# Where a batch's rank products stand: one in each product's tail, or four in a row behind the last

## The reference

```python
x = x + (x @ W0.T + b0) + 2 * ((x @ A0[id0]) @ B0[id0])        # rank 16
x = x + (x @ W1.T + b1) + ((x @ A1[id1].T) @ B1[id1].T)        # rank 16
```

## Time and profile before

| | us |
|---|---|
| median of 3 runs (lowest, highest) | 282.63 (282.19, 282.70) |
| the profiled execution | 281.97 |
| its span | 280.4 |
| TensorE busy (matmuls, 1321) | 276.3 |
| VectorE busy (321) | 214.5 |
| ScalarE busy (141) | 102.0 |
| granted TensorE clock, mean of the span | 0.999 of full |

### The profile page before, as it was taken

How to read it: one execution, slowest core, us unless ns; L and a number is a source line. 1 busy time by engine, 2 the same in 40 slices (tenths; PEclk the granted TensorE clock), 3 DMA queues, 4 the chain that set the end, 5 groups by cost and what they waited for, 6 DMA issues and landing times.

```text
span 280.4 us, 3861 instructions
## 1 busy us (share of the span) xinstructions
PE 276.3 (99%) x1321; PEld 225.4 (80%) x1321; DVE 214.5 (77%) x321; ACT 102.0 (36%) x141; POOL 19.2 (7%) x45
## 2 busy tenths in 40 slices
PE   8999999999999999999999999999999999999995
PEld 6888888888888886888877888888877888888885
DVE  5779999999899799798972875875772865875413
ACT  4665465352964665404131223132311223132000
POOL 3333200400000001001000000000000000000000
PEclk9999999999999999999999999999999999999999
DMA  7997100200476200383702703703802302203003
GB/s 245 388 411 287 37 1 2 57 19 0 150 269 247 86 2 19 109 314 126 248 15 84 247 29 121 240 6 124 236 1 86 125 0 112 95 2 132 19 0 150
DMA packets 13112, 33.93 MB, mean 121 GB/s; under 512 B 2165, under 2 KB 2421, under 8 KB 13094
## 3 DMA queue, kind: packets, MB, share of 16 engines
q1 hardware_dynamic: 12066, 31.60, 31.8%
q0 software_dynamic: 1024, 2.10, 2.3%
q10 hardware_dynamic: 4, 0.00, 0.0%
HBM read 22.09 MB, written 11.60 MB: 120 GB/s over the span
## 4 chain that ended last, share of the span: by engine, by line
PE 99%; DVE 0%; issue 0%
PE bank L1291 18%; PE bank L1292 18%; PE bank L1293 18%; PE bank L1127 9%; PE bank L1131 9%; PE bank L1132 9%; PE bank L1323 3%; PE bank L1298 3%; PE bank L1159 1%; PE bank L1161 1%; PE bank L1160 1%; PE bank L1147 1%; PE bank L1146 1%; PE bank L1145 1%; PE bank L1170 1%; PE bank L1238 1%
## 5 line engine op out<-in xcount | busy, mean ns | idle before, releaser
L1291 PE MATMUL bank<-ops,late 128*128 128x512 f32 x192 | 75.1, 391 | 0.0
L1292 PE MATMUL bank<-ops,late 128*128 128x512 f32 x192 | 74.8, 390 | 0.0
L1293 PE MATMUL bank<-ops,late 128*128 128x512 f32 x192 | 74.7, 389 | 0.0
L1131 PE MATMUL bank<-ops 128*128 128x512 f32 x112 | 43.8, 391 | 0.0
L1132 PE MATMUL bank<-ops 128*128 128x512 f32 x112 | 43.6, 390 | 0.0
L1291 PEld LDWEIGHTS bank<-ops,late 128*128 128x128 f32 x192 | 36.1, 188 | 8.7 <-issue 1.2
L1293 PEld LDWEIGHTS bank<-ops,late 128*128 128x128 f32 x192 | 36.0, 188 | 7.6
L1292 PEld LDWEIGHTS bank<-ops,late 128*128 128x128 f32 x192 | 36.1, 188 | 7.4
L1127 PE MATMUL bank<-ops 128*128 128x512 f32 x112 | 40.9, 400 | 0.0
L525 ACT CAST late<-rows 128x512 fp32r<-128x512 f32 x24 | 14.7, 620 | 54.7 <-DVE rows L823 29.5
L1127 PEld LDWEIGHTS bank<-ops 128*128 128x128 f32 x112 | 21.5, 192 | 4.7 <-DVE ops L707 0.3
(11 more groups left out here) (175 smaller groups left out, 397.4 us busy)
## 6 DMA issues: line engine op xcount, KB each, us to landing
out<-raw_a SPq DMA_DIRECT2D x27, 256.0 KB, 2.3
raw_a<-xT SPq DMA_DIRECT2D x10, 512.0 KB, 6.8
a<-rb_rows SPq DMA_DIRECT2D x8, 392.0 KB
x_mid<-xT SPq DMA_DIRECT2D x6, 512.0 KB, 6.3
raw_b<-W SPq DMA_DIRECT2D x2, 1024.0 KB, 16.2
rb_rows<-b_hl SPq DMA_DIRECT2D x3, 512.0 KB
rb_rows<-late SPq DMA_DIRECT2D x3, 512.0 KB
raw_b<-V SPq DMA_DIRECT2D x4, 256.0 KB, 3.7
```

The source lines that it names most:

```text
L1131: mm(bank[:, :], left(u, 0, k, m), op_k(v, 1, k), start=False, stop=False, skip_group_check=on_top)
L1291: mm(bank[:, :], hi, t_op(t, 0, k), start=(start and k == 0), stop=False, skip_group_check=not start)
L1292: mm(bank[:, :], hi, t_op(t, 1, k), start=False, stop=False, skip_group_check=not start)
L1293: last = mm(bank[:, :], lo, t_op(t, 0, k), start=False, stop=(k == KH - 1), skip_group_check=not start)
```

## The change

In batches 0 to 6 the rank products of V and W leave the ends of p4 and p3. The order becomes: product p4, product p3, `stacked`, then the rank products X, V, Z, W, then p1 of the next batch. In the last batch it is product p4, `stacked`, X, V, Z, `p3_last`. The semaphores p_done[3] and p_done[4] are now given by the rank products in their new place. No other engine's list is changed.

```diff
                 product(b, S4, B22, W, True)
+
+            def fill_w(b):
                 ranks(b, 0, 1, W).then_inc(p_done[3], 1)
...
                 product(b, A22, T4, V, True)
-                stacked(b)
+
+            def fill_v(b):
                 ranks(b, 1, 0, V).then_inc(p_done[4], 1)
...
                 p4(b)
+                if b + 1 < B:
+                    p3(b)
+
+                stacked(b)
                 fill_x(b)
+                fill_v(b)
                 fill_z(b)
                 if b + 1 < B:
-                    p3(b)
+                    fill_w(b)
                 else:
                     p3_last()
```

## The result

| | before | after |
|---|---|---|
| median, us (lowest to highest) | 282.43 (282.10 to 282.70) | 284.46 (283.94 to 285.14) |
| ratio, 95% interval | | 1.0076 (1.0062 to 1.0090) |
| profiled execution, its span | 281.97, 280.4 | 285.14, 283.5 |

The change makes the kernel slower, by 2.0 us between the medians and 2.15 by the ratio; forecast was +2.35 and 285.0. The profiled execution is the longest of the six. Timed again in another series the ratio was 1.0061 (1.0048 to 1.0075), or +1.7 us.

A forecast was written before the change was run, and what follows sets the result against it. TensorE, busy 99% of the span, bounds the kernel. Seven stalls at p1, +2.5 us, less 0.15 for passages saved, make +2.35 on a median of 282.63: 285.0 us forecast, range 283.4 to 286.2.

The forecast's parts named there:

- What bounds the kernel, and where the wait comes: TensorE, busy 99% of the span, bounds; p1 waits at seven seams for X's copy, 0.36 us each, 2.5 in all.
- The copy: ScalarE's copy out of X: starts 0.43 us after X's rank product starts, takes 0.587, release 0.04 to 0.05.
- T: The start of X's rank product, from which each seam's times are counted; p1's first matmul was due 0.92 us later.
- Load to matmul: At p1 after the wait: time from weight load to its matmul, bounded by 0.19 and 0.23 us.
- The load passes the wait: Rival at p1: weight load runs ahead of the wait, p1 0.15 us late, +0.9 in all, 283.5; chance 0.14.
- A matmul after a pause has a slow second: Rival at p1: each new pause costs 0.12 us more, +3.2 in all, 285.8; chance 0.14.
- The passage saved: One passage fewer between full and rank products per batch: 0.02 us each, 0.15 won in all, ends 0 and 0.35.
- No stall, not slower: Rival at p1: ScalarE frees X before the copy's recorded end, only 0.15 us won, 282.5; chance 0.05.
- The covers: Later VectorE, ScalarE and SP work stays hidden: 3.7 us spare before p7, 0.1 at first seam's p2(1), load_x(4) in time.

The follow-up runs named there:

- x_early: Changed kernel with X's rank product alone put back in front of p3, V, Z and W behind it: 282.63 us, ratio 1.0008.
- v_early: Changed kernel with V's rank product back at the end of p4, X, Z, W behind p3: 285.93 us, ratio 1.0125.
- x_last: Changed kernel with the rank products ordered V, Z, W, X in batches 0 to 6: 289.35 us, ratio 1.0250.
- p6_first: Changed kernel, but from batch 1 on p6 comes before p1 and p5 before p2: 282.55 us, ratio 1.0009.
- half_copy: Changed kernel, but the copy of X takes only the first 256 of 512 columns: 283.22 us, ratio 1.0032.
- x_in_p3: Changed kernel with X's rank product inside p3, before its last quarter, V, Z, W behind p3: 282.67 us, ratio 1.0013.
- before_again: The kernel before, unchanged, timed as a version of its own: 282.42 us, ratio 0.9997.

## Why the prediction was right

- *What bounds the kernel, and where the wait comes* held: a stall at p1 of batches 1 to 7 and nowhere else in the loop. x_early, in which only V, Z and W are late, had no slower beat.
- *The copy* was sized from rows of before to the hundredth: start at T + 0.43, 0.587 long, release within 0.05.
- *Load to matmul* is the mis-sized term: I put 0.19 to 0.23, from the load's length and from the start phase. It measured 0.11 (196.48 to 196.59), the same in v_early and x_last, where the second matmul again stands 0.34 behind the first. So a stall is 0.26, not 0.36, and the seven are 1.8 us, not 2.5. The forecast of +2.35 lies 0.2 to 0.65 over the two measurements, and 0.55 over the 1.8 that the seams account for.
- *Some of the nearness is luck.* In the first series 0.36 us of the 2.15 lies outside the seams, in the start phase, of which the prediction said nothing; it hides more than half of the overestimate. The forecast of 285.0 also stood on a median of 282.63, 0.2 over the 282.43 of six runs.
- Two of my rivals were halves of this one thing. "The load passes the wait" gave T + 1.07, which is where the matmul's row starts; but the load's row starts there as well, not before, so it did not pass. "A matmul after a pause has a slow second" gave 0.12 more, which is the 0.11 by which the first row is longer. Added, 0.15 + 0.12 = 0.27, they are the stall. I had priced the second on top of a full load, which counted the load twice. The earlier trace rows already showed the right term: a first row of 0.50, the second matmul 0.35 behind.
- *The passage saved* (0.02 a batch, 0.15 in all) is 0.01 in the beat of p6_first, and no time showed it.
- *No stall, not slower*: refuted. The load starts 0.05 behind the copy's recorded end. In this order on TensorE the stall goes down only with half the columns, to 0.05.
- *The covers* held. In the first seam

```profile
136.79 0.62 ACT L525 CAST late<-rows 128x512 fp32r<-128x512 f32 x1
...
137.31 0.58 ACT L538 COPY raw_a<-bank 128x512 f32<-128x512 f32 x1
...
138.30 0.39 PE L1291 MATMUL bank<-ops,late 128*128 128x512 f32 x1
```

keep_p1(1) ends at 137.89 and p2(1) starts on time at 138.30. With release and load, 0.16, there were 0.25 us to spare; I had 0.1, as I let copy follow cast without overlap. But it is the stall of p1(1) that makes this room: in x_early, without a stall, p2(1) is due at 137.24 and its load waits for the same copy. load_x(4) was issued at 138.01 and the h products ran on without a wait.

What stays open is the phase ahead of the loop. p4(0) ended at 127.7 and 128.0 in the two profiles of before, and between 127.8 and 129.1 in the nine others, whose order on TensorE is the same up to there. The ratios lie 0 to 0.6 us above what the beats account for, in every version but before itself. Two places stand out in the profiles. At about 45 us TensorE's loads stood idle 0.2 to 1.0 us, for nothing that the profile names, in six of the nine (0.74 in the changed kernel, 1.01 in half_copy, 0.80 in x_in_p3), but not in p6_first, v_early and x_last, nor in the two of before. At about 110 us the first h products waited 0.4 to 1.6 us for a tile of VectorE (L851) in seven of the nine, and 0.45 in before_again. So neither pause comes with every version, and one comes with before too. Whether their frequency is chance or goes with the program's later part was not settled. It is small beside the 1.8 us, which the seams show by themselves.

## What to carry to other kernels

When instructions are grouped, ask first who reads the group's results and who overwrites them: an instruction may have been standing where it stood to give a copy its time. The stall can be worked out before it is seen: start of the producer to start of the copy, the copy, the release and the part of a weight load that no matmul covers, less what is queued between. On an engine that the profile shows busy nearly all the time, look for such pauses in the weight loads and in the starts, not in the busy share.

## What the hardware showed that I had not expected

After a wait a weight load of 128 columns, 0.19 us long by its row, kept its matmul back by 0.11 only: load and matmul rows start together (196.48), the matmul's row is 0.50 instead of 0.39 long, and the stream runs from 196.59. When the pause was short, in half_copy, the load started at 175.79, the matmul's row at 175.86, 0.42 long, and the next load at 175.90: again 0.11. The Trainium skill, TensorE: Matmul & The Clock Gate, section "Architectural detail: the array is 16× 32×32, not 1× 128×128", says that a matmul can begin before its weight load is complete; the 0.11 for a load of 0.19 agrees with it, though no run here separates that from a load that is over sooner than its row. The load rows give a hint for the latter: 0.188 us for 128 columns and 0.110 for the 32 of an h product are 0.81 ns a column, and by that, as an estimate, 128 columns take 0.10 us and the rest of the row is the same for both.
